# Spreading slot numbers and probabilities by four wide products in place of sixteen narrow ones

## The reference, cut to what matters

```python
q = (x @ Wq + bq).reshape(-1, 8, 128)
q1, q2 = q[..., :64], q[..., 64:]
s1 = einsum('bhc,hnc->bhn', q1, keys[:, 0]);  s2 = einsum('bhc,hnc->bhn', q2, keys[:, 1])
s1t, i1 = top_k(s1, 8);  s2t, i2 = top_k(s2, 8)
all_scores = (s1t[..., :, None] + s2t[..., None, :]).reshape(-1, 8, 64)
all_idx = (i1[..., :, None] * 256 + i2[..., None, :]).reshape(-1, 8, 64)
scores, best = top_k(all_scores, 8)
indices = take_along_axis(all_idx, best, axis=-1)
inner = einsum('bd,bhkd->bhk', x, w_down[indices])
vals = relu(inner) * softmax(scores, axis=-1)
out = einsum('bhk,bhkd->bd', vals, w_up[indices])
```

## Time and profile before

| | |
|---|---|
| median of 3 runs | 2603.11 us (2601.43 to 2609.05) |
| the profiled execution's own time | 2612.62 us |
| its span, first to last instruction | 2610.8 us |
| busy: PE, DVE, ACT, POOL | 85%, 56%, 28%, 40% of the span |
| the `mem_*` stage's loop over tiles | from about 1585 us to the end |

### The profile page before, as it was taken

The page is one execution under the profiler, slowest core; times in us unless marked ns, Lnnn a source line. Parts: engine busy times, 40 slices in busy tenths (PEclk is TensorE's granted clock), DMA queues, the critical chain, the costliest instruction groups (busy, mean ns, idle before and its releaser), DMA issues.

```text
span 2610.8 us, 29611 instructions
## 1 busy us (share of the span) xinstructions
PE 2223.4 (85%) x10300; PEld 1263.6 (48%) x10300; DVE 1453.7 (56%) x3917; ACT 742.2 (28%) x1837; POOL 1034.6 (40%) x886
## 2 busy tenths in 40 slices
PE   3999989999499999999999997888878888788643
PEld 2666656676244444444565674444434444444200
DVE  3765665643466630000133547777877778678775
ACT  1346231121010001100134523434334343343222
POOL 0036877773111100000000005655656566566775
PEclk9999999999699999999999999889989898898755
DMA  9944145557847760043202417989989899899998
GB/s 299 289 113 134 2 82 113 126 117 162 218 138 192 194 152 2 9 131 108 59 1 32 149 45 259 342 306 333 345 308 346 316 325 342 306 332 337 349 385 347
DMA packets 242915, 531.73 MB, mean 204 GB/s; under 512 B 103774, under 2 KB 105173, under 8 KB 238611
## 3 DMA queue, kind: packets, MB, share of 16 engines
q0 software_dynamic: 170032, 379.99, 44.1%
q1 hardware_dynamic: 64413, 144.24, 18.5%
q10 hardware_dynamic: 8330, 5.71, 0.8%
HBM read 493.10 MB, written 48.92 MB: 208 GB/s over the span
## 4 chain that ended last, share of the span: by engine, by line
PE 67%; DVE 19%; DMA 7%; issue 3%; ACT 2%; POOL 2%; SPq 0%; POOLq 0%; DVEq 0%; ACTq 0%
PE bank L1154 13%; PE bank L1131 5%; PE bank L987 4%; PE bank L998 4%; PE bank L1493 4%; PE bank L1476 4%; PE bank L1484 3%; PE bank L1363 3%; PE bank L748 3%; PE bank L650 3%; PE bank L671 3%; PE bank L1141 2%; PE bank L658 2%; DMA stage<-xn_d 2%; PE bank L874 2%
## 5 line engine op out<-in xcount | busy, mean ns | idle before, releaser
L1334 POOL DMA_INDIRECT qv<-in_L_ffn_rows,qv x162 | 160.7, 992 | 754.6 <-DVE qv L1749 645.0
L1639 ACT ACTIVATE stage<-stage,qv 128x32 f32<-128x32 f32 x640 | 204.6, 321 | 471.5 <-DVE ring_more L1859 124.0
L310 POOL DMA_INDIRECT adj<-e_cnt,e_idx x80 | 166.4, 2080 | 211.4 <-issue 186.7
L1476 PEld LDWEIGHTS bank<-stage,big 128*128 128x128 f32 x1280 | 173.5, 202 | 98.6 <-issue 72.0
L1334 POOL DMA_INDIRECT big<-in_L_ffn_rows,qv x160 | 162.6, 1016 | 112.3 <-PE bank L1493 74.2
L1476 PE MATMUL bank<-stage,big 128*128 128x125 f32 x1280 | 184.9, 291 | 23.4 <-ACT stage L1606 22.8
L1334 POOL DMA_INDIRECT ring_more<-in_L_ffn_rows,qv x159 | 160.2, 1008 | 106.6 <-PE bank L1493 70.0
L310 POOL DMA_INDIRECT adj_b<-e_cnt,e_idx x80 | 169.0, 2112 | 52.4 <-issue 27.4
L1334 POOL DMA_INDIRECT h<-in_L_ffn_rows,qv x159 | 160.5, 1009 | 48.5 <-issue 45.1
L1154 PE MATMUL bank<-big,wreg 125*125 125x512 f32 x400 | 172.0, 592 | 0.0
L1154 PE MATMUL bank<-big,qv 125*125 125x512 f32 x400 | 171.8, 592 | 0.0
(11 more groups left out here) (259 smaller groups left out, 4019.7 us busy)
## 6 DMA issues: line engine op xcount, KB each, us to landing
wreg<-in_L_gnn_basis SPq DMA_DIRECT2D x30, 1024.0 KB, 5.6
stage<-in_L_gnn_basis POOLq DMA_DIRECT2D x45, 512.0 KB, 4.9
big<-in_L_mix_W SPq DMA_DIRECT2D x4, 4096.0 KB
adj<-adj_b POOLq DMA_DIRECT2D x9, 1328.1 KB, 25.8
adj<-wreg SPq DMA_DIRECT2D x5, 2187.5 KB
adj_b<-wreg SPq DMA_DIRECT2D x5, 2187.5 KB
wreg<-adj SPq DMA_DIRECT2D x10, 1093.8 KB
qv<-adj SPq DMA_DIRECT2D x10, 1093.8 KB
```

The lines of the kernel that those rows point to most:

```text
L310: nc.gpsimd.indirect_dma_start(out=(adj, adj_b)[g % 2], out_offset=bass.IndirectOffsetOnAxis(ap=e_idx[:, g:g + 1], axis=0), in_=e_cnt[:, g ...
L1334: nc.gpsimd.indirect_dma_start(out=ring[place(t, s)], out_offset=None, in_=a["L0_ffn_rows"], in_offset=bass.IndirectOffsetOnAxis(ap=slots_ ...
L1476: mm = nc.tensor.matmul(psum[F_BANKS[n % 2]][:, 0:P], w1_sb[:, k, 128 * n:128 * n + 128], y1_t[:, k, :], start=(k == 0), stop=(k == KC - 1))
L1639: nc.scalar.activation(wsel[:, s % DRING, :], mask, ACT.Relu, scale=inner[:, s:s + 1]).then_inc(p_diag, 1)
```

## The change

`spread_slots` had sixteen products for a spread: for each column group g and each e, a 125x32 matrix that picks the rows of group g, times 16 numbers. Now DVE first writes a wider copy of the 64 numbers, four times 64, in which the copy for group g holds zeros on all partitions outside of that group (`widen`, one multiplication by `groups`, 125x4 of 0 and 1). Then one product for each e with `mask` (a 0/1 matrix that adds up the four groups) spreads all 64 numbers. The same numbers land in PSUM. `widen` is called behind L1744 and behind L1758, and waits for what these write; `groups` is made once, with `selx` and `mask`.

```diff
@@ -206,6 +206,8 @@
         slot_f = view(qv, 832, [SLOTS], P)
+        wide_f, wide_p = (view(qv, 9600 + 4 * SLOTS * n, [4, 4, SLOTS // 4], P) for n in range(2))
+        groups = view(qv, 9600 + 8 * SLOTS, [4], P)
...
@@ -1505,20 +1507,19 @@
-            def spread_slots(bank, what):
-                for g in range(4):
-                    for e in range(4):
-                        mm = nc.tensor.matmul(psum[bank][WIDE * e:WIDE * e + WIDE, 16 * g:16 * g + 16], selx[:, g, 0:WIDE],
-                                              what.rearrange("p (s e) -> p e s", e=4)[:, e, :], start=True, stop=True, skip_group_check=True)
+            def spread_slots(bank, wide):
+                for e in range(4):
+                    mm = nc.tensor.matmul(psum[bank][WIDE * e:WIDE * e + WIDE, 0:SLOTS], mask[0:P, :],
+                                          wide[:, e, :, :].rearrange("p g s -> p (g s)"), start=True, stop=True, skip_group_check=True)
                 return mm
 
             def behind(t):
 
                 pe.wait_ge(p_found, 2 * t + 1)
-                spread_slots(3, slot_f).then_inc(p_found_pe, 1)
+                spread_slots(3, wide_f).then_inc(p_found_pe, 1)
                 yield
                 pe.wait_ge(p_found, 2 * t + 2)
-                spread_slots(4, prob.rearrange("p h k -> p (h k)")).then_inc(p_found_pe, 1)
+                spread_slots(4, wide_p).then_inc(p_found_pe, 1)
                 yield
                 pe.wait_ge(p_slots, 2 * t + 1)
                 spread_x(t, 0)
@@ -1546,7 +1547,7 @@
...
-            pe.wait_ge(p_sel, 2)
+            pe.wait_ge(p_sel, 3)
...
@@ -1681,7 +1682,12 @@
                 for _ in later:
                     pass
 
-        TOPN = 4 * PKH + 2 + 2 * PKH + 4 + 6 + 2
+        TOPN = 4 * PKH + 2 + 2 * PKH + 4 + 6 + 1 + 3
+
+        def widen(to, what):
+
+            return nc.vector.tensor_tensor(to, what.rearrange("p (s e) -> p e s", e=4).unsqueeze(2).to_broadcast([P, 4, 4, SLOTS // 4]),
+                                           groups.unsqueeze(1).unsqueeze(3).to_broadcast([P, 4, 4, SLOTS // 4]), ALU.mult)
 
         def top(dve, t):
 
@@ -1741,7 +1747,10 @@
             dve.wait_ge(p_top, n)
             if t:
                 dve.wait_ge(p_found_pe, 2 * t - 1)
-            nc.vector.scalar_tensor_tensor(slot_f, pick_a, float(NKEYS), pick_b, ALU.mult, ALU.add).then_inc(p_found, 1)
+            nc.vector.scalar_tensor_tensor(slot_f, pick_a, float(NKEYS), pick_b, ALU.mult, ALU.add).then_inc(p_top, 1)
+            n += 1
+            dve.wait_ge(p_top, n)
+            widen(wide_f, slot_f).then_inc(p_found, 1)
             yield
 
             def slots_taken():
@@ -1755,7 +1764,9 @@
             dve.wait_ge(p_top, n + 1)
             nc.vector.reciprocal(prob_s, prob_s).then_inc(p_top, 1)
             dve.wait_ge(p_top, n + 2)
-            nc.vector.tensor_tensor(prob, prob, prob_s.unsqueeze(2).to_broadcast([P, PKH, TOPK]), ALU.mult).then_inc(p_found, 1)
+            nc.vector.tensor_tensor(prob, prob, prob_s.unsqueeze(2).to_broadcast([P, PKH, TOPK]), ALU.mult).then_inc(p_top, 1)
+            dve.wait_ge(p_top, n + 3)
+            widen(wide_p, prob.rearrange("p h k -> p (h k)")).then_inc(p_found, 1)
             for _ in range(5):
                 yield
             if t:
@@ -1871,6 +1882,8 @@
             nc.vector.tensor_copy(selx.rearrange("p g (e m) -> p g e m", e=4),
                                   ident[0:P, :].rearrange("p (g m) -> p g m", g=4).unsqueeze(2).to_broadcast([P, 4, 4, WIDE])).then_inc(p_sel, 1)
             nc.vector.tensor_reduce(mask, ident[:, :].rearrange("p (g m) -> p m g", g=4), AX, ALU.add).then_inc(p_sel, 1)
+            nc.vector.tensor_reduce(groups, ident[0:P, :].rearrange("p (g m) -> p g m", g=4), AX, ALU.add).then_inc(p_sel, 1)
+            dve.wait_ge(p_sel, 3)
             dve.wait_ge(m["ln2"], ADDS["ln2"] + (2 + RSQ) * PRE + TOPK)
             normed(dve, 1)
             for _ in finish(0):
```

More of the change, by code:

```diff
@@ L1658, in mem_act @@
             exps(0)
-            act.wait_ge(p_sel, 2)
+            act.wait_ge(p_sel, 3)
             spread_x(0, 0)
```

## The result

| | before, same comparison | changed |
|---|---|---|
| median (lowest to highest), 6 runs each | 2602.27 us (2597.62 to 2609.05) | 2630.25 us (2617.44 to 2644.86) |
| ratio, 95% interval | | 1.0115 [1.0092, 1.0138] |

The change made the kernel slower by 28.0 us. That is outside of the range of 2599 to 2615, on the side to which the forecast gave 0.19. The profiled execution is the lowest of the six, 2617.44 us. Its part ahead of the memory layer, which the change doesn't touch, was about 18 us shorter than in the profiled execution of before: tile 0's first spread began at 1554.6 us, and at 1572.57 in before. So I compare from that spread to the end: 2615.6 - 1554.6 = 1061.0 us against 2610.8 - 1572.6 = 1038.2, which is 22.8 more. The other 5 us between this and the medians are not seen in these two executions.

What follows compares the result with a forecast made beforehand. Nothing is full, so the chain of waits sets a tile's length. 1.15 us lasting from tiles 0 to 7 plus 0.88 for tile 9's rows made 2.0, taking 2603.1 to 2605.1 us; range 2599 to 2615.

Steps and rivals of the forecast that it cites:

- the side to which the forecast gave 0.19: Whole run beyond 0.3% slower: 0.13 from the lower clock, 0.06 from the dear end of nothing being returned.
- the granted clock still at 1.00 behind the first spread: Expected in the profile: PE keeps its full clock after waiting for the slot numbers; 0.5 there would prove the forecast wrong.
- PE falls to 1.2 GHz at the spread: Rival, chance 0.15: slower rows and L1484 products add 1.8 us per tile; 2624 unreturned, some 2608 if it shrinks.
- about 0.6: Granted clock behind the first spread from which the lower-clock rival was to decide.
- The widening: DVE multiplication of 125x256, two per tile: 0.42 us each, bounds 0.22 and 0.69; the pair adds 0.88 to the chain.
- What lasts: Tiles 0 to 7: of 0.71 us more on the chain in each of eight tiles, 1.15 us lasts, not 5.7.
- A displacement shrinks to 0.38: From tile to tile a delay falls to 0.38 of itself or less, as later tiles get the full clock sooner.
- Nothing is handed back: Rival, chance 0.15: each tile's delay lasts in full, 6.9 us, 2610.0; 2616 with widenings near 0.69.
- both widenings and no cover: At the search's end both widenings lie directly on the chain; the dot, ACT and PE's rows stand behind them.
- the second spread: PE's spread of the probabilities: 0.20 us on the chain for 0.37, giving 0.17 back, at most 0.29.
- the first spread's own saving: PE's spread of the slot numbers: gives nothing in tiles 0 to 8, as it isn't on the chain.
- One of the prediction's signs of being wrong: The forecast is wrong if the spread's time depends on records more than on columns.

Runs made afterwards that it cites:

- e4: Changed kernel with the wide copies laid out in source order, so DVE reads 64 numbers in a row and PE picks every fourth: 2619.44 us, 1.0062.
- e8: e4 with the second widening moved behind the next dot: 2622.0 us, 1.0061.
- e1: Changed kernel with both widenings kept and waited for, but the old sixteen products reading the unwidened numbers: 2635.05 us, 1.0114.
- e6: Changed kernel with only the slot numbers widened; the probabilities are spread by the old sixteen products: 2617.44 us, 1.0050.
- e9: Changed kernel with slot numbers spread by the old sixteen products, probabilities widened in source order behind the next dot, then four products: 2601.86 us, 0.9981.
- e7: Changed kernel with only the probabilities widened; the slot numbers are spread by the old sixteen products: 2606.29 us, 1.0008.
- e5: Kernel before with two idle products ahead of the first spread, the control of e3: 2604.65 us, 0.9992.
- e3: Changed kernel with two products whose result nobody reads ahead of PE's wait for the first spread, tiles 1 to 9: 2618.04 us, 1.0051.
- x2: e3 with the idle products of w2 added: 2578.38 us, 0.9893.
- e2: Changed kernel with widening done for tile 0 only; later tiles spread tile 0's widened numbers, so the output differs: 2606.95 us, 1.0018.
- w1: Kernel before with idle products ahead of three waits of the scores and the MLP: 2586.1 us, 0.9926.
- w2: w1 with five more idle products at two waits at a tile's beginning, in the attention: 2565.35 us, 0.9856.
- w3: w2 with two idle products behind each group of four rows in tiles 8 and 9: 2570.38 us, 0.9881.

## Why the prediction was wrong, point by point

**The step that failed** is "the granted clock still at 1.00 behind the first spread". Its price was there, as the rival "PE falls to 1.2 GHz at the spread", with 0.15 and 2624 unreturned. The argument against it was that the clock is 1.00 behind a wait of 1.64 us. But the change lengthens just that wait, and behind 2.10 (e4, e8) and 2.28 us (e1, e6) the clock was some 0.6 in nearly every tile. A row at one wait was taken as evidence for a longer one. The wait's length does not decide alone: behind 2.28 us the clock stayed at 1.00 in one tile of eight (the changed kernel and e6), and behind 1.71 (e9) and 1.91 (e7) it fell once. The prediction named the row that spoke for the rival, 0.50 behind longer waits in tile 8, and gave it too little weight. The bound from which it was to decide, "about 0.6", was met: 0.59 to 0.63. But even unreturned the rival's price, 21 us, is under the 28.0 measured, and it has no term for the second fall.

The rule that the prediction cited beside that rival (the Trainium skill, TensorE: Matmul & The Clock Gate, section HAM oscillation: gaps between bursts send TensorE back to the lower clock) pointed the right way: 0.59 behind 2.28 us, 1.00 behind 1.64. The waits in that section's own example are longer than these, so what the page shows by itself didn't settle this case.

**How the loss is made up.** A mean step is 2.60 longer. By steps with the same pattern of falls, first the kernels whose chain is no longer than before (before, e5, e9), then e7 (0.4 us longer) and the others:

| clock from 36 to 48 us | clock from 94 to 105 us | steps |
|---|---|---|
| 1.00 | 1.00 | 105.27, one (before); 105.23 and 105.32 (e9); 105.64, one (e5) |
| 0.87 to 0.89 | 1.00 | 105.5 to 105.9, six (before) |
| 1.00 | 1.00 | 105.75 to 106.21, four (e7) |
| 1.00 | 1.00 | 106.37, mean of five (e3); 106.01, one (changed) |
| 1.00 | 0.84 | 106.37 (changed), 106.7, mean of three (e4) |
| 0.86 | 1.00 | 108.3, two (e3) |
| 0.86 | 0.84 | 109.2 to 109.3, four (changed); 108.1, three (e6) |
| 0.72 | 0.84 | 108.61 (changed), 108.4, mean of four (e4) |

Against the 105.8 of before, e3's steps without a fall are about 0.6 us longer. But at 105.8 the kernel before has its own early fall; against steps of that chain without a fall (105.2 to 105.6) they are 0.7 to 1.1 longer, for a chain that is 1.06 longer. By this comparison most or all of the delay is paid, and the early fall that is missing in e3 and e7 makes up for a part of it.

The fall behind the first spread, which the rival priced at 1.8, costs 0 to 1.0 within its own step. The second fall, some 50 us later, goes with 1.7 to 2.9 more in the step. No step of the prediction has it. Where the stretch has 0.86 (the changed kernel, e1, e3, e7), the eight L1455 products take 5.41 us, not 3.71, which is 1.70 of it. Where the fall begins earlier (e4 with 0.72, the three tiles of e6 with 108.1), they take 3.71, and the loss lies elsewhere. In the changed kernel's commonest kind of step, 109.27 on the average of four, the longer chain (1.06), the slower rows (0.87) and these products (1.70) make 3.63, where 3.5 is measured against 105.8; that this sum comes out nearly right is no proof of each term.

The second fall comes in five of seven steps of the changed kernel, in all of e1, in four of seven of e4, e6 and e8, and in two of seven of e3, where the first one is gone. That the fall at the spread makes it more frequent is what these counts suggest. How it does so, and why it lies later than in the kernel before, stays open: in tiles of the changed kernel with and without it PE's waits between 26 and 46 us are the same to 0.1 us (1.30, 0.6, 0.5 and 0.7 us), and no run was made on that alone.

**The widening** was mis-sized: 0.607 us, not 0.42, within the bounds (0.22 to 0.69). The shape was right, but it reads every fourth number; in order it takes 0.425 (e4). This term adds 0.37 us to a tile's chain. It isn't what decided: e4, without it, is slower too (1.0062), though by about half.

**What lasts** was wrong as a rule. "A displacement shrinks to 0.38" was read from three tiles with steps that differ by 0.5 us. For 0.4 us more on the chain the step is again 105.8 (e7). For some 1.06 us, 0.6 lasts in each tile even at the full clock at both places (e3), and 1.4 where PE is at 2.4 GHz nearly throughout (x2). What returns a displacement is less time at half clock, as the prediction said: these tiles of e7 and e3 lack the early fall. But that is limited. "Nothing is handed back" was nearer than the forecast.

**What was right.** The chain's path with both widenings and no cover; 20 widenings; the second spread at 0.15 where 0.20 was said, within the cap of 0.29 on its gain; that the first spread's own saving does not reach the end (e2). One of the prediction's signs of being wrong did show: both forms of a spread stream 256 columns, sixteen times 16 or four times 64, and with a quarter of the records the time fell from 0.37 to 0.15. So between these two the records set the time more than the columns. The estimate came near because it went by the rows' equal number of records. The overhead for each matmul that the prediction cites from the Trainium skill (TensorEngine Tiling (Array Packing), section Performance Considerations) was counted there once for each record; counted once for each product it gives, as an estimate, 0.40 and 0.10 us, close to the 0.37 and to the 0.11 or 0.12 that the four products took at the full clock (x2, e2).

## What to carry to other kernels

Work that is moved from TensorE to VectorE ahead of a TensorE instruction is to be priced twice: by its own time on the chain, and by the clock that TensorE has behind the longer wait; a trace that shows full clock behind the present wait does not vouch for a longer one, so give that case the weight of a step, not of a rival. Before saving records on TensorE, look at the granted clock by stretch: here 24 records fewer for each spread were worth nothing measurable, and products without a use at the right waits 1.4%. These must be tried at each wait: they gained where the lower clock lay on the path (w1, w2), and nothing where it was full already (e5) or where PE doesn't set the pace (w3).

## What the runs showed of the hardware

- 0.64 us more of waiting (2.28 for 1.64) took TensorE from a granted clock of 1.00 to some 0.6 behind the wait, in seven of eight tiles (the changed kernel, e6). The place of the work was the same. Two idle products in the wait brought it back to 1.00 (e3).
- A multiplication of 125x256 in fp32 on VectorE took 0.607 us with a source read at every fourth number, 0.425 in order.
- Four products of 64 columns on four strips took 0.15 us on the chain (0.11 in x2), sixteen of 16 columns 0.37, for the same 256 columns.
- What a fall of the clock cost hung on the products that it lay on: the last eight of the attention took 5.41 us at 0.57 (changed kernel), and 3.71 before, where a fall of nearly the same mean (0.87 for 0.86 in the 12 us) was over by then.
- A tile's length gathers in groups, by which stretches fall to the lower clock: 105.3 to 105.9 us before; 106.0 to 106.9, 108.1 to 108.6 and 108.9 to 109.5 with the longer chain (e1, e3, e4, e6, e8, changed).
